# Relational loop of a four-layer graph network: turns of five groups with three fetched and two picked, in place of six with four fetched

## What is computed

```python
h = jnp.maximum(_layernorm(x, axis=-1), 0.0)
h_src = feat[src]                       # feat is h
msg = jnp.zeros((h_src.shape[0], weight.shape[2]), dtype=feat.dtype)
for r in range(num_rels):               # 16
    mask = etypes == r
    msg = msg + h_src * mask[:, None].astype(feat.dtype) @ weight[r]
out = jax.ops.segment_sum(msg, dst, num_segments=feat.shape[0])
x = x + out
```

## Time and profile before

| | us |
|---|---|
| median of 3 runs | 2324.14 (2319.7 to 2330.75) |
| the profiled execution | 2326.9 |
| its span, first to last instruction | 2325.1 |

### The profile page before, as it was taken

One profiled execution on the slowest core, in us unless ns is written; L12 is line 12 of the kernel. 1 busy time (PEld: TensorE's weight loads), 2 busy tenths in 40 slices (PEclk: granted clock), 3 DMA queues, 4 the chain that ended last, 5 costly groups with the idle time before them and its releaser, 6 DMA issues. The chain is left out here.

```text
span 2325.1 us, 34869 instructions
## 1 busy us (share of the span) xinstructions
PE 1782.0 (77%) x8596; PEld 854.9 (37%) x8597; DVE 1680.0 (72%) x4253; ACT 1225.2 (53%) x2361; POOL 1109.2 (48%) x1007
## 2 busy tenths in 40 slices
PE   2777776845888788878887885688968897789676
PEld 0222223522444344434443445333333333333244
DVE  7999995353566565556655654999889988999654
ACT  6777774122333333333433341489838993899411
POOL 1000000026666665666665662378927893689500
PEclk9999998977989999999999995699968997999877
DMA  5000001021111111111111113000000000000000
GB/s 163 0 0 0 0 0 68 1 52 27 36 29 29 29 30 32 30 29 29 34 29 29 29 36 93 1 0 1 1 1 1 1 0 1 1 1 1 14 1 15
DMA packets 29627, 50.61 MB, mean 22 GB/s; under 512 B 12820, under 2 KB 13826, under 8 KB 29054
## 3 DMA queue, kind: packets, MB, share of 16 engines
q0 software_dynamic: 17664, 18.12, 4.8%
q1 hardware_dynamic: 11890, 31.59, 4.4%
HBM read 36.58 MB, written 7.39 MB: 19 GB/s over the span
## 5 line engine op out<-in xcount | busy, mean ns | idle before, releaser
L800 POOL DMA_INDIRECT adj<-h_table,l_idx x544 | 557.6, 1025 | 317.2 <-issue 158.2
L990 DVE TENSOR_SCALAR adj<-adj,node_key 125x1024 f16<-125x1024 f16 x825 | 371.9, 494 | 355.5 <-PE psum L935 166.0
L1565 POOL TENSOR_TENSOR gat_ring<-gat_ring,adj 125x750 f32<-125x750 f32 (+2 forms) x375 | 503.2, 1346 | 202.4 <-ACT gat_ring L1630 197.6
L935 PE MATMUL psum<-adj,x_sb 125*128 125x512 f16 x1650 | 445.1, 412 | 161.9 <-DVE adj L990 149.8
L863 ACT ACTIVATE l_z<-psum 128x320 f32<-128x320 f32 x204 | 88.9, 436 | 492.7 <-remote 259.1
L1453 DVE SCALAR_TENSOR_TENSOR gat_ring<-x_sb,gat_node,psum 125x750 f32<-125x750 f32 (+2 forms) x375 | 319.3, 863 | 19.6 <-ACT x_sb L1592 9.5
L1627 ACT ACTIVATE gat_ring<-gat_ring,gat_node 125x750 f32<-125x750 f32 (+2 forms) x339 | 278.8, 822 | 68.1 <-DVE gat_ring L1453 64.4
L1703 PE MATMUL psum<-gat_ring,gat_hx 125*65 125x500 f32 (+1 forms) x500 | 261.6, 617 | 57.3 <-POOL gat_ring L1565 55.5
L935 PEld LDWEIGHTS psum<-adj,x_sb 125*128 125x128 f16 x1650 | 161.8, 103 | 382.3 <-DVE adj L990 196.2
L378 PE MATMUL psum<-col_hot,src_hot 128*128 128x500 bf16 x808 | 205.4, 376 | 110.3 <-DVE src_hot L307 89.7
L1421 DVE SCALAR_TENSOR_TENSOR psum<-adj,gat_node,psum 125x750 f32<-125x750 f16 (+1 forms) x276 | 259.2, 939 | 1.3
(11 more groups left out here) (247 smaller groups left out, 2075.5 us busy)
## 6 DMA issues: line engine op xcount, KB each, us to landing
adj<-h_table,l_idx POOLq DMA_INDIRECT x544
adj<-key_table SPq DMA_DIRECT2D x33, 250.0 KB
adj<-adj SPq DMA_DIRECT2D x3, 1662.5 KB
adj_saved<-adj SPq DMA_DIRECT2D x1, 3840.3 KB
adj<-adj_saved SPq DMA_DIRECT2D x5, 688.2 KB
x_sb<-in_x SPq DMA_DIRECT2D x1, 781.2 KB
x_saved<-x_sb SPq DMA_DIRECT2D x1, 781.2 KB
out<-x_sb SPq DMA_DIRECT2D x5, 156.2 KB
```

The lines of the kernel that those rows point to most:

```text
L800: pool.indirect_dma_start(out=to[:, t, :], out_offset=None, in_=table[:, :], in_offset=bass.IndirectOffsetOnAxis(ap=index[:, t:t + 1], axi ...
L935: last = pe.matmul(psum[:, PAIR[half] + t, :], h_parts[:, k, :], select[0:P, k % SELECTS, t * GE:(t + 1) * GE], start=(k == 0), stop=(k == ...
L990: v.tensor_scalar(select[0:P, k % SELECTS, :], keys, node_key[:, k:k + 1], None, ALU.is_equal).then_inc(s_sel, 1)
L1565: pool.tensor_tensor(slot, slot, adj[:, k, cols(c)], ALU.mult).then_inc(s["weight_ready"], 1)
```

## The change

A turn takes five groups instead of six: positions 0, 1 and 3 are fetched (12 gathers in place of 16), positions 2 and 4 picked. 205 groups make 41 turns. TensorE's node tiles are spread 4, 6, 4, 6, 5 over the positions, the relations 3, 3, 4, 3, 3. With five positions the parity of a group changes from turn to turn: its PSUM bank is (half + position) % 2, and the one-hots get a fourth slot and a list of slots over ten groups. `pair_pick`, the picked rows, gets a tile of its own. The last turn is now an even one, and the loops' bounds and the written-out turns follow. DVE's order of selects, one-hots, windows and waits is written anew for five positions; ScalarE copies the indices at position 3 instead of 4.

```diff
-SIX = 6
+FIVE = 5
-OFFSETS = (0, 1, 4, 2, 3, 5)
-FETCHED = {0: 0, 1: 1, 3: 2, 4: 3}
-PICKED = {2: 0, 5: 1}
+OFFSETS = (0, 1, 3, 2, 4)
+FETCHED = {0: 0, 1: 1, 3: 2}
+PICKED = {2: 0, 4: 1}
+FG = len(FETCHED)
+HOT_SLOTS = (0, 1, 2, 0, 1, 2, 0, 1, 2, 3)
...
-        pair_pick = carve(2 * GT * 2 * D).rearrange("p (k t d) -> p k t d", k=2, t=GT)
+        pair_pick = sb("l1_pair_pick", [128, 2, GT, 2 * D], FP16, l1_scope)
...
-        PARTS = ((0, 3), (3, 6), (6, 9), (9, 11), (11, 14), (14, R))
+        PARTS = ((0, 3), (3, 6), (6, 10), (10, 13), (13, R))
+        SHARES = ((0, 4), (4, 10), (10, 14), (14, 20), (20, NT))
...
-                        for k in range(4):
-                            pool.wait_ge(s_z, SIX * (j - 1) + FREED[k])
+                        for k in range(FG):
+                            pool.wait_ge(s_z, FIVE * (j - 1) + FREED[k])
...
-                            if pos == 4 and indexed:
+                            if pos == 3 and indexed:
                                 indices(j)
...
-                        slot, bank = pos % 3, pos % 2
+                        slot, bank = hot_slot(half, pos), (half + pos) % 2
...
-                            last = pe.matmul(psum[0:D, SUMS[half], 0:SIX * W], rel[:, r, :],
+                            last = pe.matmul(psum[0:D, SUMS[half], 0:FIVE * W], rel[:, r, :],
...
-                        for pos, lo, hi in ((0, 0, 4), (1, 4, 8), (2, 8, 12), (3, 12, 18), (4, 18, 22), (5, 22, NT)):
-                            z(j, pos)
+                        for pos in range(FIVE):
+                            z(j, pos, half)
                             if not static(j, LAST):
-                                pick(j, half, lo, hi)
+                                pick(j, half, *SHARES[pos])
...
                         selects(j, half, 6, 8)
-                        hots(j, 2)
                         window(j, 1, half)
                         selects(j, half, 8, 10)
+                        hots(j, 2, half)
                         window(j, 2, half)
                         selects(j, half, 10, 12)
-                        hots(j, 3)
+                        pause_after_selects(j, 12)
+                        selects(j, half, 12, 14)
+                        hots(j, 3, half)
                         pause_after_hots(j, 3)
-                        selects(j, half, 12, 14)
+                        selects(j, half, 14, 16)
                         window(j, 3, half)
```

More of the change, by code:

```diff
@@ L756, in gnn @@
                 "picked_T_copied", "picked_turned"))
-        s_got = [sem(f"l1_gathered{k}", l1_scope) for k in range(4)]
+        s_got = [sem(f"l1_gathered{k}", l1_scope) for k in range(FG)]
         s_first = [sem(f"l1_first_rows{k}", l1_scope) for k in range(2)]
@@ L971, in _, with hots @@
                     link = Chain(dve, s_gc)
-                    def hots(j, pos):
-                        n = SIX * j + pos
+                    def hots(j, pos, half):
+                        n = FIVE * j + pos
                         if not (isinstance(j, int) and n < 3):
@@ L1020, in turn @@
                         selects(j, half, 2, 4)
-                        hots(j, 1)
+                        hots(j, 1, half)
                         pause_after_hots(j, 1)
@@ L1060, in _ @@
                     turn(2, 0)
-                    with nc.Fori(1, LAST // 2, engines=[ENG.DVE], head_slot={ENG.DVE: 0}) as q:
+                    with nc.Fori(1, LAST // 2 - 1, engines=[ENG.DVE], head_slot={ENG.DVE: 0}) as q:
                         turn(2 * q + 1, 1)
                         turn(2 * q + 2, 0)
-                    turn(LAST, 1)
-                    for j, half in ((LAST - 1, 0), (LAST, 1)):
-                        bases = [base_of(j, pos) for pos in range(SIX)]
-                        for pos in range(SIX):
+                    turn(LAST - 1, 1)
+                    turn(LAST, 0)
+                    for j, half in ((LAST - 1, 1), (LAST, 0)):
+                        bases = [base_of(j, pos) for pos in range(FIVE)]
+                        for pos in range(FIVE):
                             add_window(j, pos, bases[pos], half)
```

117 lines of the change are left out of this document (57 added, 60 removed).

## The result

The changed kernel takes 2369.64 us (median of 4 runs, 2365.6 to 2373.05) where the kernel before takes 2323.95 (4 runs, 2319.7 to 2330.75): a ratio of 1.0194, interval 1.0178 to 1.021. It is 45.7 us slower; +14.4 was forecast. The direction was right, the size was not.

What follows compares the result with a forecast made beforehand. Bound: TensorE's signals held late during gather runs. Turn 0 42.3 + 39 x 21.8 + last turn 15.4 = 907.9 against 893.5, +14.4, so 2338.5 us; forecast's own range 2311 to 2366, wider range 2270 to 2430.

Steps and rivals of the forecast that it cites:

- What bounds the kernel: Relational loop: TensorE's completion signals arrive late during unbroken gathers, until 1.50 us after the last; 6.5 of 25.8 us lost.
- TensorE's turn, 18.5: TensorE's own pace in the new turn: one position less, 19.3 - 0.81 = 18.5 us.
- POOL 15.5 a turn, no bound: POOL's 12 gathers at 1.29 us take 15.5 us a turn, where before 20.6, so POOL can't be the bound.
- selects lock POOL out: Rival, slower: DVE selects hold up each gather, a run of eight 3.2 us longer; turn 25.0, time 2463 us; chance 0.02.
- Turn 0, 42.3; last turn, 15.4: The relational loop's ends: turn 0 falls from 49.8 to 42.3 us; the last, one position less, takes 15.4.
- The steady turn, 21.8: Each of 39 middle turns takes 21.8 us, the middle of 22.2 (from tile 14) and 21.4 (from tile 16).
- The walk: Steps through a new turn from position 0's matmuls: first gather 1.46, eight gathers 11.8, release 13.3, first new picks 14.25 us.
- early hold: Rival, slower: hold begins with the gather run, TensorE stops before tile 12; turn 24.6, time 2447.7 us; chance 0.12.
- late hold: Rival, faster: TensorE gets to tile 18 before it starves; turn 20.5, time 2287.8 us; chance 0.15.
- Loss in proportion to gathers: Rival, slower: the turn's loss scales with gathers, 6.5 x 12/16 = 4.9; turn 23.4, time 2400.9 us; chance 0.15.
- Break-even, 21.43 a turn: Steady turn at which the change neither gains nor loses: (893.5 - 57.7) / 39 = 21.43 us.

Runs made afterwards that it cites:

- the run of ten fills a group: Changed kernel without gathers from turn 2 on, ten small GpSimd fills in place of each group's four gathers: 2191.9 us, kernel before 2308.7 on that chip.
- the gates: Changed kernel with the three groups refetched after products 0, 2, 4 (2456.8 us) or 1, 1, 3 (2530.3 us), instead of 0, 1, 3; kernel before 2329.2.
- The pause behind group 0: Changed kernel with three small GpSimd fills, each waited for, behind group 0's gathers only: 2282.2 us, 0.9877 of the kernel before.

## Why the prediction was wrong in size

**What bounds the kernel.** Right in the cause, short in the account. The loss comes with the gathers: without them the turn is TensorE's own; with POOL busy but nothing gathered too; with each run cut, most of it is gone. But it is waits and, for 1.4 of its 4.6 us, slower matmuls, which the prediction did not reckon with. That the signals pass 1.5 us behind the run's end is borne out in the long turn shown (1046.12 to DVE's select at 1047.65), but "announced together" was too simple: in the long turn above, some come through one at a time within the run (1040.48, 1041.89).

**TensorE's turn, 18.5.** 18.54 on the chip without late signals, 18.0 with no gathers at all. Right within 0.5.

**POOL 15.5 a turn, no bound.** Right for the changed kernel; on the chip without late signals its twelve gathers fit into 18.54. The further lengthening by selects, 0.03 a gather, did not come: 1025 ns on average in both kernels, so 0.24 too much a turn. A gather does lengthen beside DVE: in the changed kernel's trace 83 gathers with no DVE instruction beside them take 944 ns, the 373 beside a select 1049 on average. The rival *selects lock POOL out* would have shown as up to 0.49 a gather, and falls.

The rule behind that rival, of the Trainium skill's page SBUF — State Buffer, section Who interferes with whom, is seen in the gathers' durations only as that 0.1 us. GpSimd's fills agree with it better: in the run of ten fills a group, the 106 with no DVE instruction beside them take 0.21 us each, and those beside a select 0.21 to 0.57.

**Turn 0, 42.3; last turn, 15.4.** 42.1 and 12.9. The first right, the second 2.5 too high: what the last turn saves is more than a position.

**The steady turn, 21.8.** This is the step that failed. Measured 22.62, 39 x 0.82 = 32.0 us, which with -0.2 and -2.5 of the ends is, within 0.2, the whole way from +14.4 to the stage's +43.5. The walk as far as the first new picks was good: 14.25 us from position 0's product, where the long turn shown has 1048.59 - 1034.62 = 13.97. What it had wrong is how many tiles TensorE has behind it by then, and how often such a turn comes:
- "Position 1 is long done when group 0 is issued, so the run of eight stays." Group 1 follows group 0 in 25 of 39 turns, with 22 runs of seven or eight, not 39. In the short turn shown the signal of position 1 arrives behind group 0's last gather, POOL pauses, and the turn is 20.57.
- "The hold should begin about 4 to 7 us into the run", after a rest of over 2 us, with tile 14 or 16 the first to be picked behind it. In the long turn shown it begins at about the run's third gather, after a rest of 2.73, and TensorE stops before tiles 8, 10 and, briefly, 12; the picks after the release start from tile 12, not from tile 14 or 16. That is the rival *early hold* (24.6; measured 24.9). The 1.54 of rest in the earlier trace rows had been read as the cause of a later hold, on one turn.

So two rivals came true by turns, *early hold* in 16 turns and *late hold* in 16, the latter in outcome (20.5) and not by its mechanism: in 10 of these groups 0 and 1 do not follow each other at all, and the short turn shown stops before tile 8 as the long one does. My 21.8, a middle of tile numbers, came near 22.6 by luck, without describing either kind. Some luck was also in the walk's first term: 1.46 from the product to the first gather took ScalarE's copy (1030.67) for the product's end. By the earlier trace rows it was 1031.41 - 1028.86 = 2.55 in the kernel before; in the new turn it came out at 1036.13 - 1034.62 = 1.51. And tile 14 would have been due at 11.5 by the prediction's own positions, not 11.3; nothing rests on that. The prediction looked at three turns of the kernel before, all with an eight, and did not ask whether the order of group 1's gate and group 0's end could tip.

**Loss in proportion to gathers.** Its turn, 23.4, is as far from 22.62 as mine, 0.8 on the other side, and the loss itself is near it: 4.6 where it had 4.9. It falls as a mechanism by the gates, which change the loss at a fixed number of gathers.

**Break-even, 21.43 a turn.** The pause behind group 0 passes below it, at 20.4, and its kernel is faster than the kernel before; the changed kernel at 22.6 is slower. The formula holds.

## What to carry to other kernels

Where an engine's waits are put down to "remote" and end together behind a burst of indirect gathers, look at the bursts' lengths in every turn, not in one: a wait that used to separate two bursts may now be met already. A pause of 1.2 to 1.35 us on the issuing queue behind every burst, three a turn, made this kernel about 5% faster (by ratios from different chips) at the cost of one small fill each. It also made that queue the bound, so add up its own work before making a pause longer. A pause in one place alone gave a part of this here and nothing in the kernel before, where the bursts closed up elsewhere. And before turns are made smaller, multiply TensorE's own pace by the number of turns: here that alone cost 69 us.

## What the runs showed of the hardware

- Late signals go with the chip, or with its state at the time. In six of the seven sets of runs, each on one chip, the kernel before took 2307 to 2329 us; in the other, 2188.8 (2184.9 to 2192.5, 7 runs), and no signal was late there, not even under twelve gathers in a row. Worked out from that time, with turn 0 some 15 us shorter as the changed kernel's was, the kernel before has turns of about 22 there, near POOL's own 20.6; this is an estimate, as its trace was not taken on that chip, nor was the changed kernel run on it without another edit.
- It takes gathers, not a GpSimd busy with fills: 18.05 a turn under ten fills a group, 18.0 under none.
- A gather that follows another starts 0.30 behind it; one that follows a fill that was waited for, 0.94 behind it. That is most of the pause. One that had to wait for TensorE's product starts 0.79 behind the product's modelled end in most cases (1035.34 to 1036.13).
- The granted clock falls behind TensorE's stops: 0.50 from 1048.70 on, after stops of 2.31, 1.91 and 0.44 us, and over whole stages 1.00 with 0.04 us of standing still a turn, 0.95 with 3.27, 0.86 with 5.33. It falls without late signals too: with six fills behind each group, on the chip without late signals, TensorE stands still 5.45 us a turn for source rows, and the granted clock is 0.90.

Open: what in the gathers delays the signals, GpSimd's work on them or their transfers, which no run separates, and why one chip is free of it; why eights of groups 1 and 2 cost so little; and what made six turns short although groups 0 and 1 followed each other.
